# Layer 3's query norm: squares in PSUM, a block transpose and block sums on VectorE, one folding product per head, and query pieces made a step earlier

## What is computed

```
q = (hidden_states @ q_proj_w.T).reshape(B, Q, NUM_HEADS, HEAD_DIM).transpose(0, 2, 1, 3)   # 32 heads of 128
k, v = ...                                                        # 8 key/value heads, repeated 4 times
q = rmsnorm(q, q_norm_w)      # q * rsqrt(mean(q*q over the 128 of a head) + 1e-5) * w
k = rmsnorm(k, k_norm_w)
scores = einsum('bhqd,bhkd->bhqk', q, k) / sqrt(128) + attention_mask
attn = softmax(scores);  out = einsum('bhqk,bhkd->bhqd', attn, v)
return out.reshape(B, Q, 32 * 128) @ o_proj_w.T
```

## Time and profile before

| | |
|---|---|
| time, median of 3 runs | 2904.11 us (2902.35 to 2905.36) |
| span of the profiled execution, which is its own time here | 2904.7 us |
| PE busy | 2778.9 us, 96% of the span |
| PE weight loads | 2337.4 us, 80% |
| DVE, ACT, POOL busy | 1728.2, 1048.6, 826.4 us |
| chain of work that ended last | PE 90%, DVE 6%, ACT 2%, issue 2% |
| TensorE's granted clock, mean | 0.984 of full |

### The profile page before, as it was taken

One profiled execution on the slowest core, in us unless ns is written; L12 is line 12 of the kernel. 1 busy time (PEld: TensorE's weight loads), 2 busy tenths in 40 slices (PEclk: granted clock), 3 DMA queues, 4 the chain that ended last, 5 costly groups with the idle time before them and its releaser, 6 DMA issues.

```text
span 2904.7 us, 47006 instructions
## 1 busy us (share of the span) xinstructions
PE 2778.9 (96%) x14928; PEld 2337.4 (80%) x14928; DVE 1728.2 (59%) x3969; ACT 1048.6 (36%) x2828; POOL 826.4 (28%) x708
## 2 busy tenths in 40 slices
PE   7997999999999998889999999999999999999998
PEld 5875888888888886667888888778878888888886
DVE  5756545544644646667777777745552555555557
ACT  3542333333333332124444444321123444444442
POOL 4011432432442431322222222245522222212200
PEclk8998999999999999999999999999999999999999
DMA  4001111111110110111111111012111000001000
GB/s 145 12 12 53 41 44 33 47 36 32 47 41 28 51 44 19 45 30 33 30 30 30 31 31 30 26 41 58 58 45 40 27 27 26 27 26 27 29 5 30
DMA packets 59826, 106.35 MB, mean 37 GB/s; under 512 B 7184, under 2 KB 11536, under 8 KB 59536
## 3 DMA queue, kind: packets, MB, share of 16 engines
q1 hardware_dynamic: 56448, 96.49, 11.6%
q10 hardware_dynamic: 3216, 7.81, 0.8%
HBM read 100.09 MB, written 2.10 MB: 35 GB/s over the span
## 4 chain that ended last, share of the span: by engine, by line
PE 90%; DVE 6%; ACT 2%; issue 2%; DMA 0%; POOL 0%; ACTq 0%; DVEq 0%; POOLq 0%
PE four L587 51%; PE outp L587 23%; PE value L587 9%; PE turned L930 4%; PE turned L709 1%; DVE stats L1565 1%; DVE xt_lo L1594 1%; PE turned L634 0%; DVE nt L1537 0%; DVE nt L1539 0%; DVE probs L1589 0%; DVE x L1767 0%; DVE x L1973 0%; ACT sq L1317 0%; ACT vc L1203 0%
## 5 line engine op out<-in xcount | busy, mean ns | idle before, releaser
L558 POOL TENSOR_TENSOR w_hi<-raw,zero 128x512 fp32r<-128x512 f32 x347 | 371.8, 1072 | 1926.3 <-PE four L587 896.4
L1767 DVE SCALAR_TENSOR_TENSOR x<-outp,g_inv,x 128x512 f32<-128x512 f32 x768 | 556.6, 748 | 383.5 <-PE outp L587 383.2
L562 POOL TENSOR_TENSOR w_lo<-raw,w_hi 128x512 fp32r<-128x512 f32 x352 | 454.0, 1290 | 32.3 <-ACT w_hi L1203 5.1
L587 PE MATMUL four<-xt_hi,w_lo 128*128 128x512 f32 x1024 | 424.8, 415 | 16.8 <-DVE xt_lo L1594 12.0
L587 PE MATMUL four<-xt_hi,w_hi 128*128 128x512 f32 x1024 | 406.2, 397 | 0.0
L587 PE MATMUL four<-xt_lo,w_hi 128*128 128x512 f32 x1024 | 404.4, 395 | 0.0
L587 PE MATMUL outp<-w_hi,a_lo 128*128 128x512 f32 x800 | 330.3, 413 | 14.3 <-DVE x L1767 7.5
L1203 ACT ACTIVATE pT<-turned 128x512 f32<-128x512 f32 x320 | 191.6, 599 | 345.1 <-PE turned L930 287.3
L587 PE MATMUL outp<-w_hi,a_hi 128*128 128x512 f32 x800 | 316.0, 395 | 0.0
L587 PE MATMUL outp<-w_lo,a_hi 128*128 128x512 f32 x800 | 315.3, 394 | 0.0
L1396 ACT ACTIVATE probs<-probs,top 128x128 f32<-128x128 f32 x512 | 199.6, 391 | 237.6 <-DVE top L1810 126.7
(11 more groups left out here) (259 smaller groups left out, 4627.9 us busy)
## 6 DMA issues: line engine op xcount, KB each, us to landing
raw<-in_stream SPq DMA_DIRECT2D x352, 256.0 KB, 2.6
ctx_raw<-in_ctx_t ACTq DMA_DIRECT2D x4, 512.0 KB, 6.2
x<-in_x_in ACTq DMA_DIRECT2D x2, 1024.0 KB, 11.9
kz<-kT SPq DMA_DIRECT2D x32, 64.0 KB, 2.3
pb<-in_position_bias ACTq DMA_DIRECT2D x1, 2048.0 KB, 8.7
out<-x SPq DMA_DIRECT2D x8, 256.0 KB, 2.0
qw<-in_qweight ACTq DMA_DIRECT2D x1, 768.0 KB, 3.9
ln_w<-in_ln_weight ACTq DMA_DIRECT2D x1, 256.0 KB, 2.7
```

The lines of the kernel that those rows point to most:

```text
L558: pool.tensor_tensor(w_hi[:, k, :], raw[:, k % RAW, :], zero[:, :].to_broadcast([P, D]), ALU.add)\
L562: pool.tensor_tensor(w_lo[:, k, :], raw[:, k % RAW, :], f32(w_hi[:, k, :]), ALU.subtract)\
L587: m = pe.matmul(out_, l, r, start=start, stop=stop, skip_group_check=True)
L1767: dve.scalar_tensor_tensor(out=x[:, b, :], in0=O[no_f(k) % 2][:, :], scalar=scale, in1=x[:, b, :], op0=ALU.mult, op1=ALU.add)\
```

## The change

A piece's squares are now made by ACT in place, in the piece's own PSUM bank, after the copy to `qT`. DVE then transposes that bank in blocks of 32x32 into `sq` and adds up each run of 32 columns (`query_turn`), which leaves 16 partial sums per partition in `part`; after the second half of a head, one PE product with a constant 0/1 matrix `fold` adds the four blocks that belong together, for both halves at once (`q_squares`, 128x32 output into that half's own bank). DVE picks the block that belongs to its partition with a 0/1 mask `own` and runs one inverse root of 128x8 for the whole head, 13 small operations in the odd steps, in place of 12 in every step. The query pieces are made one step earlier: step k makes half `1 - t` of head `(k + 1) // 2 + 1`; the piece (head 1, half 0) goes into the prologue.

```
@@ prologue
-            self.first += [q[0], norm[5], v[7], norm[6], norm[7], q[1]]
+            self.first += [q[0], norm[5], v[7], norm[6], norm[7], q[1], ("q", 1, 0)]
@@ parts / pieces
-            return [("q", t, 0, KT - 1), ("q", t, KT - 1, 1)]
+            return [("q", 1 - t, 0, KT - 1), ("q", 1 - t, KT - 1, 1)]
+    def made_head(self, i):
+        return (i + 1 if self.name == "L2" else i) // self.U + 1
+    def sums_head(self, i):
+        h = (i + 1) // 2
+        return h if i % 2 and 0 < h < self.heads else 0
@@ PE: a bank of J is free for the next piece
-                    if n == 2 and no > 1 and by_no[no - 1][0] == "q":
-                        pe.wait_ge(s["newton"], at(L, lambda i: newton_base(
-                            L, by_no[L.piece[what_f(i)] - 1]) + 1, k, it))
+                    if n == 2 and no > 2 and by_no[no - 2][0] == "q":
+                        pe.wait_ge(s["q_turned"], at(L, lambda i: L.rstd[by_no[L.piece[what_f(i)] - 2]] - 2 * B,
+                                                     k, it))
+                        if by_no[no - 2][2] == 1:
+                            pe.wait_ge(s["newton"], at(L, lambda i: newton_base(
+                                by_no[L.piece[what_f(i)] - 2][1]) + 1, k, it))
@@ PE: sums of squares
-                def q_squares(what_f, k, it):
-                    pe.wait_ge(s["sq"], at(L, lambda i: L.rstd[what_f(i)], k, it))
-                    bank_ = J[(L.piece[what_f(k)] + 1) % 2][:, :]
-                    for j in range(4):
-                        m = mm(bank_[:, 2 * j:2 * j + 2], buf["sq"][:, tokens(j)], ones[:, :], True, True)
-                    m.then_inc(s["qss"], 1)
+                def q_squares(head, k, it):
+                    pe.wait_ge(s["sq_sums"], at(L, lambda i: 2 * B + 2 * head(i) + 2, k, it))
+                    bank_ = piece_bank(L, ("q", head(k), 1))
+                    mm(bank_[:, 0:32], buf["fold"][:, :], buf["part"][:, :, :].rearrange("p t c -> p (t c)"),
+                       True, True).then_inc(s["qss"], 1)
@@ PE: step
                     if 1 <= k <= L.NU:
                         turn(k - 1, it)
+                    if n == 2 and L.sums_head(k):
+                        q_squares(L.sums_head, k, it)
...
-                    if n == 2:
-                        for what in L.pieces(k):
-                            q_squares(lambda i: L.pieces(i)[0], k, it)
@@ ACT: leave_bank
-                    if kind == "q" and n == 2:
-                        squares(what_f, src, k, it)
...
                     copy(dst, src, scale).then_inc(s["j_out"], 1)
+                    if kind == "q" and n == 2:
+                        act.activation(src, src, ACT.Square).then_inc(s["sq"], 1)
@@ DVE
+                def query_turn(what_f, k, it):
+                    idx = at(L, lambda i: L.rstd[what_f(i)] - 2 * B, k, it)
+                    dve.wait_ge(s["sq"], at(L, lambda i: L.rstd[what_f(i)], k, it))
+                    if L.rstd[what_f(k)] > 2 * B + 1:
+                        dve.wait_ge(s["sq_sums"], at(L, lambda i: L.rstd[what_f(i)] - 1, k, it))
+                    dve.transpose(buf["sq"][:, :], piece_bank(L, what_f(k))).then_inc(s["q_turned"], 1)
+                    dve.wait_ge(s["q_turned"], idx)
+                    if what_f(k)[1]:
+                        dve.wait_ge(s["qss"], at(L, lambda i: what_f(i)[1], k, it))
+                    dve.tensor_reduce(buf["part"][:, what_f(k)[2], :],
+                                      buf["sq"][:, :].rearrange("p (c t) -> p c t", t=32), AX_X, ALU.add)\
+                        .then_inc(s["sq_sums"], 1)
...
                     if L.has_V(k):
                         dve.wait_ge(s["a_hi"], at(L, lambda i: i - L.lag_v + 1, k, it))
...
+                    if n == 2 and L.pieces(k):
+                        query_turn(lambda i: L.pieces(i)[0], k, it)
                     tail_stats(k)
```

More of the change, by code:

```diff
@@ L386, in build @@
             A2["qk_w"] = sb("qk_w", [P, 2], F32, st)
+            A2["fold"] = sb("fold", [P, P], F32, st)
+            A2["own"] = sb("own", [P, 4], F32, st)
+            A2["part"] = sb("part", [P, 2, 16], F32, st)
+            A2["pick"] = sb("pick", [P, 8, 4], F32, st)
         with ExitStack() as st:
@@ L503, in half, with newton_base @@
             return slice(t * HALF, (t + 1) * HALF)
-        def newton_base(layer, what):
-            return (RSQRT + 1) * B + RSQRT * (layer.rstd[what] - 1 - 2 * B)
+        def newton_base(h):
+            return (RSQRT + 1) * (B + h)
         def chunk_no(layer, what):
@@ L890, in attention @@
                         turn_keys(by_no[L.piece[what] - KEY_LAG])
-                    if n == 2 and what[0] == "q":
-                        q_squares(lambda i: what, 0, None)
+                    if n == 2 and what == ("q", 1, 0):
+                        pe.wait_ge(s["consts"], 5)
+                        q_squares(lambda i: 0, 0, None)
                 def scores(k, it):
@@ L1709, in query_rstd @@
+                STEPS = RSQRT + 2
+                def query_rstd(head, k, it, steps=(0, STEPS)):
+                    src = piece_bank(L, ("q", head(k), 1))[:, 0:32].rearrange("p (g c) -> p g c", c=4)
+                    rq = buf["rq"][:, 2 * (head(k) % 2):2 * (head(k) % 2) + 2, :].rearrange("p t j -> p (t j)")
+                    base = at(L, lambda i: newton_base(head(i)), k, it)
                     for j in range(*steps):
                         if j == 0:
-                            dve.wait_ge(s["qss"], at(L, lambda i: L.rstd[what_f(i)] - 2 * B, k, it))
@@ L1712, in query_rstd @@
-                            o = dve.tensor_scalar(nt[:, 0, 0:4], src, P * EPS, None, ALU.add)
+                            dve.wait_ge(s["qss"], at(L, lambda i: head(i) + 1, k, it))
+                            o = dve.scalar_tensor_tensor(
+                                out=buf["pick"][:, :, :], in0=src, scalar=P * EPS,
+                                in1=buf["own"][:, :].unsqueeze(1).to_broadcast([P, 8, 4]),
+                                op0=ALU.add, op1=ALU.mult)
                         else:
@@ L1745, in attention @@
                             rows(b + 1)
+                        if n == 2 and b == B - 1:
+                            query_turn(lambda i: ("q", 0, 0), 0, None)
                         norm_lo(norm, b)
-                    elif what[0] == "q" and n == 2:
-                        query_rstd(lambda i: what, 0, None)
+                    elif what == ("q", 0, 1) and n == 2:
+                        query_turn(lambda i: what, 0, None)
+                    elif what == ("q", 1, 0) and n == 2:
+                        query_rstd(lambda i: 0, 0, None)
+                        query_turn(lambda i: what, 0, None)
                 if n == 1:
@@ L1784, in small @@
                     def small(a, b=None):
-                        if n == 2 and 1 <= k <= L.NU and L.pieces(k - 1):
-                            query_rstd(lambda i: L.pieces(i - 1)[0], k, it, (a, b or a + 1))
+                        if n == 2 and L.sums_head(k):
+                            query_rstd(L.sums_head, k, it, (a, b or a + 1))
                     if k < L.NU:
@@ L1855, in through @@
                         if n == 2 and k < L.NU:
-                            add_tiles(k, it, range(2, B), lambda j: small(7 + j))
+                            add_tiles(k, it, range(2, B), lambda j: small(5 + j))
                         else:
@@ L1859, in through @@
                     elif n == 2 and k < L.NU:
-                        small(9, 11)
-                    small(11)
+                        small(7, 9)
+                    small(9, STEPS)
                     if L.has_V(k):
```

66 lines of the change are left out of this document (35 added, 31 removed).

## The result

The changed kernel takes 2957.93 us (median of 4 runs, 2956.89 to 2958.53) against 2903.28 us of the kernel before on the same chip: a ratio of 1.0188, interval 1.0173 to 1.0202, so 1.9% slower. The forecast was 2952 us, in a range of 2912 to 2980.

What follows compares the result with a forecast made beforehand. The prediction took PE, with 90% of the chain, to bound the kernel, with DVE at its heels. 2904.7 + 42 (pairs) + 8 (jumps) - 2 (ends) = 2953, against the median 2952 us, 1.6% slower; range 2912 to 2980.

Steps and rivals of the forecast that it cites:

- PE's list, less over the loop: Folding replaces sums-of-squares passes: PE's list 1.56 us shorter per pair of steps, 48 us over 31 pairs if PE never waits.
- small operations held: End of odd steps: POOL's split holds DVE's small inverse-root operations ahead of `a_lo`, 0.67 us on the even step's chain.
- pairs: Loop: an odd and an even step together take 19.2 us instead of 17.78, +1.4 us, 30 times, +42 us.
- the loop's jumps: Every eighth step: DVE's late start comes through in full, about 2.8 us, +1.4 x 6 = +8 us.
- the ends: Ahead of the loop and step 61: one more query piece fits a wait, its missing counterpart saves 2.7 us; -2 taken.
- The odd step: PE's folding product waits 1.78 us for DVE's transpose and reduction; the step takes 9.9 us.
- The even step: Output tiles wait for DVE's late additions to `x`: 8.6 us, with 0.67 for held small operations 9.3 us.
- a clock under 1.00 in the loop: Sign against the forecast: PE's granted clock drops in the loop, with PE standing still some 3 us in a pair.
- 2932: Rival, chance 0.17: POOL's splits miss the small operations, even step 8.6 us, 20 us less, total 2932 us.
- 2994: Rival, chance 0.12: the block transpose takes two passes, in both chains, 61 x 0.69 = 42 us more, total 2994 us.
- 2910: Rival, chance 0.08: only the fold waits, DVE catches up within even steps, a pair takes 17.8 us, total 2910 us.
- 2854: Rival, chance 0.08: PE's saving counts in full, partial sums ready in time, 48 us go, total 2854 us.

Runs made afterwards that it cites:

- the experiment that undid it: Against the changed kernel, three of the last four small DVE operations of an inverse root moved from ahead of `a_lo` to behind it: 2948.91 us, ratio 1.0151.

## Why the prediction was right

| step | predicted | measured |
|---|---|---|
| PE's list, less over the loop | 48 us | PE busy 41 us less (whole program) |
| block transpose | 0.69 us | 0.705 us |
| fold's wait, odd steps | 1.78 us | 1.79 us, 28 times |
| small operations held | 0.67 us | about 0.7 us |
| odd and even step | 9.9 and 9.3 us | 9.81 and 9.21 us |
| pairs | +1.4 x 30 = +42 us | +1.24 x 30 = +37 us |
| the loop's jumps | +8 us | +12 us |
| the ends | -2 us | +1 us (what is left of 50.4) |

That the total came out within 6 us is in part luck: the pairs were 5 us too high in the forecast, the jumps 4 and the ends 3 too low.

**The odd step** went as worked out, by its rows and in its cause: moving the fold alone takes the wait away, doubling the transpose lengthens it by 0.75 (to 2.52). The block transpose agrees with the estimate of 0.71 us that was made from the Trainium skill, VectorE: DVE Perf Modes, section "The three transpose paths". Between 32 and 512 columns it takes 0.705 - 0.205 = 0.50 us more, 1.04 ns a column.

**The even step** has the predicted length, but most of the wait lies elsewhere. I had PE wait at the second pair of output tiles, for the additions, and put what POOL holds on that chain. That wait is there and is the last one of the step: the doubled transpose, which stands behind `a_lo`, shows in it in full (1.05 for 0.30). But in the trace PE has by then waited 1.31 us for `a_lo` at the first output tile, which the prediction left out, and only 0.30 is left for the additions. Both chains come from the late `a_lo`, so the sum was nearly right; an edit that had only brought the additions forward would have been aimed at the 0.30. That the splits hold the small operations is as the Trainium skill has it, SBUF — State Buffer, section "Who interferes with whom": the one that found a split under way ended 0.02 us behind it (1535.89 + 0.63 = 1536.52, the split 1536.50), and so did the other behind the second (1537.89, the split 1537.87).

**The jumps** were undersized. That DVE's 2.7 us come through is right: PE waits up to 3.2 us there. In three of the six PE then runs at a granted clock of 0.50 for more than 3 us, and these steps take 12.44 to 12.78 us instead of 11.12 to 11.32. Taken together the six are 20.5 us over the 8.52 of such a step; before, they were 8.6 over. I had named a clock under 1.00 in the loop as a sign against the forecast, and did not see that with the jump coming through PE would stand still for 3 us there.

**The rivals.** The splits do hold the operations (2932 falls, and the experiment that undid it got 9 of its 20 us). The transpose is one pass (2994 falls). That only the fold waits (2910) is contradicted by the 1.31 at `a_lo`. That PE's saving counts (2854) needs the partial sums in time; its condition was put wrongly, though: at 0.39 us for both operations together, under the 0.6 I gave, the fold still waited 0.79 us and the kernel was still 0.6% slower than before, because the wait for `a_lo` and the jumps are paid all the same. In another order most of that saving comes: with the piece earlier a pair takes 16.6 us against 17.78, 1.2 of the 1.56 that PE's list is shorter, and the whole of the change's loss and 15 us besides are earned back.

Not settled: why the granted clock falls behind some of the equal waits and not behind others.

## What to carry to other kernels

A product saved on the engine that bounds the kernel can be worth nothing, as here, if its replacement is a chain through another engine that the next product waits for: before such a change, follow the chain from the last input to that wait, and count what lies between. Where a new wait appears, look first for work of the waiting engine to put in front of it; the same instructions in another order gave back 70 us here. And when operations are moved out of the way, look at which chain they stand in next: three that left `a_lo`'s took 0.30 of the 0.71 us back at the additions.

## What the runs showed of the hardware that was not expected

- A longer wait on TensorE can cost more than its length. With the transpose doubled, the granted clock fell to 0.50 behind the 2.5 us of standing still at the fold in ten of the loop's 28 odd steps, 1.58 us more for each. In the changed kernel, where that wait is 1.8 us, it did so in none of the loop's 28; with the small operations spread it did once, behind 1.86 us in the loop's first odd step (11.53 us instead of 9.8).
- TensorE pays for the hardware loop's jump too. With 8 steps a turn it shows no such wait of its own there; with 16 it came out late at both jumps, by up to 2.1, 3.3 and 3.4 us in the three kernels that had it. Fewer jumps were worth 13 and 11 us where DVE was late anyway, and cost 5 us in the kernel before.
- An operation of VectorE with one tensor in SBUF can be held as well: scaling `inv` by `gate`, 128x4, took 1.00 us under a split in the kernel with the whole piece earlier (1506.00 to 1507.00, the split ended at 1506.98), and 0.22 where none was under way.
